# A graph network on one core: the edge weights' part on VectorE from a broadcast load, and a bias row on TensorE instead of a second node table

## The chip, the core and the metric

The kernel runs on one core of one Trainium2 chip. The core has five engines that run side by side: PE (TensorE, matrix products), DVE (VectorE), ACT (ScalarE), POOL (GpSimd, which here only issues indirect DMA transfers, "gathers") and SP (SyncE, which issues the plain DMA transfers). They wait for one another by semaphores. The metric is the device time of one execution in microseconds (us); lower is better.

## The reference, cut to what matters

There are 50,000 nodes with 128 features, 25,000 edges sorted by their target, and four layers one behind the other. The change touches the first layer and the second convolution of the second layer.

```python
# first layer: ew is one number per edge
ef  = concat([x[src], x[dst], ew[:, None]])           # 128 + 128 + 1
msg = leaky_relu(ef @ W_edge + b_edge)                # slope 0.01
red = segment_sum(msg, dst)
x1  = layernorm(x + leaky_relu(concat([x, red]) @ W_node + b_node))
# second layer: two convolutions with attention, then again a residual and a layernorm
h1  = relu(conv(x1, q0, k0, v0, s0))
x2  = layernorm(x1 + conv(h1, q1, k1, v1, s1))        # conv ends with "+ h @ s_w + s_b"
```

## The kernel before

Edges and nodes are padded to 49 tiles; a tile is 512 edges and, beside them, two blocks of 512 nodes. Features lie on the 128 partitions once a block has been transposed by PE. The program is a row of stages with a barrier between them: `setup`, `layer0`, `conv` 0, `conv` 1, `layer2`, `layer3`. Each stage is a loop over 49 steps plus a few to drain, written out in full; the order of the instructions on each engine is the order in which the step function writes them, and every dependence is a semaphore wait written by hand.

**`setup`** loads the weights, computes the row numbers by which later stages gather, and prepares constants. Its DVE part ends in a chain in which each instruction waits for the one before (`link`). Line 318 centres the bias row of the second convolution (`s_b1c`, broadcast over the 128 partitions).

**`layer0`**, step `t`, with tile `now` = t and older tiles behind it:
- PE (line 602 on) transposes the node rows `xn`, then forms `psZ`, the messages before the activation, from three products: `w_src` (L614), `w_dst` (L615), and `w_edge_row` times `erow` (L616). The last one adds the edge weights' part: `erow` is a tile of zeros with the 512 edge weights in its first row, and `w_edge_row` has the weight row in its first row. Then come the transposes of the next tile's gathered rows `xd` and `xs`, the node products L624, `centred` products `psE` of `tT` (L589), `centred` of `psZ` for an older tile, and the edge products L640 and L642.
- ACT copies, squares and scales; `y01` (L696, shown as `y`) follows L642, and `z01` (L676, shown as `z` in the rows) is 0.01 times `psZ` plus a bias.
- DVE: `lr` (L712, the leaky ReLU of the products), `tT` (L717 and L721, plus the input), `msg` (L727, the leaky ReLU of `psZ`), the running sum `red` (L732), the sum of squares `var` (L441), `rstd` times a mask (L744), the output `xo` (L749), and `xb` (L756). `xb` is `xo` of the two node blocks plus `s_b1c`.
- SP loads `xn` and `erow` of coming tiles, stores `xo` to the table `x1` and `xb` to a second node table, `x1b`.
- POOL issues per step four gathers of `xs` for the tile three ahead and some 3.2 of `xd` (196 in all, 48 of them issued already in `setup`); each is one quarter of a tile.

**`conv`, layer 1** (the second convolution): `own_rows` (L940) forms `psE[k]` = h1 times `s1c` for the two node blocks, and DVE's `add_x1` (L1165) adds the residual, which SP loads from `x1b` (with the bias in it) for nodes. PE's order in a step is: transposes of `xs` and `xd`, query product, transposes of the nodes, key product (L1003), values `psV` (L953), `own_rows` for both blocks, `alike` `psA` (L958, needs DVE's `kq`), and `edge_products` (L947, L948).

Of the kernel before, what the change touches and what calls it, by code (L numbers as in the profile page):

```python
# [129 lines left out]
def setup(nc, io, h):  # L130

    with ExitStack() as ctx:
# [10 lines left out]
        dst1 = sb("dst1", [P, COLS])  # L143
        src1, src1_rows = sb("src1", [P, COLS]), sb("src1_rows", [HALF, 2 * P])
# [60 lines left out]
        def _(act):  # L205
# [10 lines left out]
            load(h.w_edge_row[0:1, :], io["w_edge_row"])  # L216
# [6 lines left out]
        def _(dve):  # L223
# [283 lines left out]
def layer0(nc, io, h):  # L507


    with ExitStack() as ctx:  # L510
# [8 lines left out]
        erow = sb("erow", [P, 2, TILE])  # L519
# [4 lines left out]
        xo, xb = sb("xo", [P, 2, 3, TILE]), sb("xb", [P, 2, 2, TILE])  # L524
        psT, psZ, psY, psE = ps("psT", 2), ps("psZ", 1), ps("psY", 3), ps("psE", 2)
        node_landed, erow_landed, node_stored, edge_stored, xb_stored = [
            [sem(f"{n}{s}") for s in range(2)] for n in (
                "node_landed", "erow_landed", "node_stored", "edge_stored", "xb_stored")]
        (e_turned, n_turned, e_kept, n_kept, erow_zero, z_ready, z01_ready, msg_ready, red_ready, yn_ready, ye_ready,
         y01_ready, lr_ready, te_ready, tn_ready, ee_ready, en_ready, ce_ready, cn_ready, sq_ready, var_ready,  # L530
         lnv_ready, rstd_ready, out_ready, xb_ready, masked, last_landed) = map(sem, (
             "e_turned", "n_turned", "e_kept", "n_kept", "erow_zero", "z_ready", "z01_ready", "msg_ready", "red_ready",
             "yn_ready", "ye_ready", "y01_ready", "lr_ready", "te_ready", "tn_ready", "ee_ready", "en_ready",
             "ce_ready", "cn_ready", "sq_ready", "var_ready", "lnv_ready", "rstd_ready", "out_ready", "xb_ready", "masked",
# [20 lines left out]
        def _(sp):  # L555
            sp.wait_ge(erow_zero, 1)
# [20 lines left out]
            for s in range(2):  # L577
                sp.wait_ge(xb_stored[s], 16 * tiles_in_slot(s))

        @block.tensor  # L580
        def _(pe):
# [18 lines left out]
            def step(t):  # L600
                soon, now, last, old = t.tile(-1), t.tile(0), t.tile(1), t.tile(2)
                if now:
# [30 lines left out]
                if old:  # L633
                    pe.wait_ge(te_ready, old.n + 1)
                    wait(pe, msg_ready, old.n + 3 if now else STEPS)
                    centred(psZ[:, 0, :], tT[:, 2, :]).then_inc(ee_ready, 1)
# [11 lines left out]
        def _(act):  # L648
# [7 lines left out]
            def step(t):  # L656
# [16 lines left out]
                if now:  # L673
                    act.wait_ge(z_ready, now.n + 1)
                    wait(act, msg_ready, now.n)
                    nc.scalar.activation(z01[:, :], psZ[:, 0, :], ACT.Identity, bias=h.x01b_edge[:, :],  # L676
# [25 lines left out]
        def _(dve):  # L702
            nc.vector.memset(erow[:, :, :], 0.0).then_inc(erow_zero, 1)

            def step(t):
                now, last, old = t.tile(0), t.tile(1), t.tile(2)
                (g, a, b), (g2, a2, b2), (g3, a3, b3) = t.group(1), t.group(2), t.group(3)
                if g:
# [5 lines left out]
                    dve.wait_ge(lr_ready, g.n + 1)  # L714
                if last:
# [7 lines left out]
                if now:  # L723
# [3 lines left out]
                    nc.vector.scalar_tensor_tensor(out=msg[:, :], in0=psZ[:, 0, :], scalar=h.col("b_edge"),  # L727
# [1404 lines left out]
```

## Time and profile before

| | us |
|---|---|
| median of three timed runs | 3164.38 (3162.36 to 3165.82) |
| the profiled execution | 3169.91 |
| its span, first to last instruction | 3168.1 |
| `layer0` in it, from the first PE instruction at 135.97 to the barrier before `conv` 0 at 679.2 | 543 |
| period of one step in `layer0` and in `conv` 1 | 10.44 and 11.34 |

| engine | busy us | share of the span |
|---|---|---|
| PE | 2503.6 | 79% |
| DVE | 2587.8 | 82% |
| ACT | 2089.9 | 66% |
| POOL | 1869.3 | 59% |

No engine bounds the whole program. Each stage has its own limit, so the stage's timeline is what is to be read: instructions in order of time, with how long the engine stood idle before one and who released it. An instruction's recorded time includes its way through the pipeline, so the next one on the engine can start some 0.1 us before the last one's recorded end.

### The profile page before, as it was taken

How to read it: one execution, taken by the hardware profiler on the slowest of the kernel's cores; microseconds unless marked ns; L12 is line 12 of the kernel's file. 1: busy time of each engine (PE TensorE's matmuls, PEld its weight loads, DVE VectorE, ACT ScalarE, POOL GpSimd, SP SyncE). 2: the span in 40 equal slices, each digit the busy share in tenths (PEclk: the TensorE clock that was granted, in tenths of full speed). 3: DMA queues.
4: the chain of work that ended last, by engine and by line, in shares of the span. 5: the costliest groups of instructions: out<-in, count | busy, mean ns of one | idle time of the engine just before them, and what ended most of it. 6: DMA issues, size and time to landing. Idle time of an engine off the chain costs nothing. (4 is left out here: it accounts for less than half of the span.)

```text
span 3168.1 us, 46332 instructions
## 1 busy us (share of the span) xinstructions
PE 2503.6 (79%) x14131; PEld 1745.7 (55%) x14131; DVE 2587.8 (82%) x3230; ACT 2089.9 (66%) x3726; POOL 1869.3 (59%) x1771
## 2 busy tenths in 40 slices
PE   7899999959999968888888699999999753345500
PEld 3466666637677756666665466777777542234400
DVE  6689999969999959999999457898888747999900
ACT  0176767746666648888888589999999744545500
POOL 4477777723344427777775556555555007777776
PEclk9999999979999989999999899999999855666855
DMA  7456767657677756777776448888988538984211
GB/s 210 114 176 222 222 217 229 214 167 219 207 215 220 216 161 209 231 233 233 232 232 206 118 138 212 217 210 206 236 213 213 153 101 275 277 275 136 81 40 39
DMA packets 495087, 611.79 MB, mean 193 GB/s; under 512 B 66865, under 2 KB 284651, under 8 KB 494716
## 3 DMA queue, kind: packets, MB, share of 16 engines
q1 hardware_dynamic: 433030, 495.63, 52.0%
q0 software_dynamic: 56480, 111.88, 13.6%
q8 instruction: 118, 1.93, 0.3%
q10 hardware_dynamic: 5334, 1.32, 0.2%
q14 instruction: 125, 1.02, 0.1%
HBM read 391.94 MB, written 220.55 MB: 193 GB/s over the span
## 5 line engine op out<-in xcount | busy, mean ns | idle before, releaser
L1848 POOL DMA_INDIRECT f_rows<-table_x,src_row x196 | 228.9, 1168 | 225.2 <-POOLq L1249 165.8
L1328 POOL DMA_INDIRECT g_xd_xs<-table_x,dst_row x196 | 199.0, 1015 | 263.9 <-PE g_psT L1396 170.1
L781 POOL DMA_INDIRECT c_xs<-table_x,src_row x196 | 187.3, 956 | 261.9 <-PE c_psT L923 209.4
L771 POOL DMA_INDIRECT c_xs<-table_h,src_row x196 | 221.3, 1129 | 121.4 <-issue 78.9
L503 POOL DMA_INDIRECT xs<-in_x,src_i x196 | 227.1, 1159 | 86.6 <-issue 55.5
L488 POOL DMA_INDIRECT xd<-in_x,dst_i x196 | 216.9, 1106 | 94.8 <-issue 47.6
L1328 POOL DMA_INDIRECT g_xd_xs<-table_x,src_row x196 | 205.0, 1046 | 59.7 <-issue 59.7
L1855 POOL DMA_INDIRECT out<-f_rows,end_i x196 | 197.1, 1006 | 62.4 <-issue 62.1
L1900 PE MATMUL f_psT<-w_ident,f_rows 128*128 128x128 f32 x196 | 48.5, 393 | 219.9 <-DVE f_rows L1993 219.9
L771 POOL DMA_INDIRECT c_xd<-table_h,dst_row x196 | 185.1, 944 | 59.7 <-issue 59.7
L1401 PEld LDWEIGHTS g_psP<-w_center,g_turns 128*128 128x128 f32 x1568 | 183.8, 191 | 49.6 <-ACT g_turns L1537 28.3
L1401 PE MATMUL g_psP<-w_center,g_turns 128*128 128x128 f32 x1568 | 197.2, 279 | 7.5 <-ACT g_turns L1566 4.7
L1032 ACT ACTIVATE c_xo<-c_pre,c_rstd 128x128 f32<-128x128 f32 x588 | 182.0, 388 | 1.6
L1900 PEld LDWEIGHTS f_psT<-w_ident,f_rows 128*128 128x128 f32 x196 | 30.9, 195 | 232.1 <-DVE f_rows L1993 232.1
L1401 PE MATMUL g_psU<-w_center,g_turns 128*128 128x128 f32 x784 | 124.7, 310 | 38.6 <-ACT g_turns L1542 25.7
L1924 ACT ACTIVATE f_sqe<-f_rows 128x512 f32<-128x512 f32 x49 | 30.9, 630 | 166.5 <-DVE f_vare L1970 146.2
L1401 PEld LDWEIGHTS g_psU<-w_center,g_turns 128*128 128x128 f32 x784 | 111.8, 220 | 46.0 <-ACT g_turns L1542 31.8
L953 PE MATMUL c_psV<-c_xsT,w_v 128*128 128x512 f32 x196 | 105.3, 619 | 35.5 <-DVE c_pv L1207 35.5
L1729 DVE TENSOR_TENSOR g_pre<-g_psP,g_xn 128x1024 f32<-128x1024 f32 x49 | 59.9, 1223 | 87.4 <-ACT g_n L1523 52.6
L1179 DVE TENSOR_TENSOR_SCAN c_m<-far,c_m,c_psA 128x512 f32<-128x512 bf16 x98 | 124.6, 1271 | 1.6 <-PE c_psA L958 1.6
L1213 DVE TENSOR_TENSOR_SCAN c_den<-c_c,c_den,c_p 128x512 f32<-128x512 f32 x96 | 122.2, 1273 | 0.0
L1219 DVE TENSOR_TENSOR_SCAN c_num<-c_c,c_num,c_pv 128x512 f32<-128x512 f32 x96 | 120.6, 1256 | 0.0
(338 smaller groups left out, 8457.2 us busy)
## 6 DMA issues: line engine op xcount, KB each, us to landing
g_share<-shares SPq DMA_DIRECT2D x196, 192.0 KB
xn<-in_x SPq DMA_DIRECT2D x49, 512.0 KB
table_x<-xo SPq DMA_DIRECT2D x49, 512.0 KB, 2.9
table_x1b<-xb SPq DMA_DIRECT2D x49, 512.0 KB, 4.9
c_xn<-table_x SPq DMA_DIRECT2D x49, 512.0 KB
table_h<-c_xo SPq DMA_DIRECT2D x49, 512.0 KB
c_xn<-table_h SPq DMA_DIRECT2D x49, 512.0 KB
c_x1r<-table_x1b SPq DMA_DIRECT2D x49, 512.0 KB
```

Source lines behind the costliest of these rows:

```text
L488: pool.indirect_dma_start(out=quarters(h.xd0[:, s, :])[j], out_offset=None, in_=io["x0"], in_offset=edge_index(h.dst_i, n, j)).then_inc(h. ...
L503: pool.indirect_dma_start(out=quarters(h.xs0[:, s, :])[j], out_offset=None, in_=io["x0"], in_offset=edge_index(h.src_i, n, j)).then_inc(h. ...
L771: pool.indirect_dma_start(out=quarters(rows[:, s, :])[j], out_offset=None, in_=table, in_offset=edge_index(columns, now.n, j)).then_inc(la ...
L781: pool.indirect_dma_start(out=quarters(xs[:, s, :])[j], out_offset=None, in_=table, in_offset=edge_index(h.src_row, now.n, j)).then_inc(sr ...
L1032: ins = nc.scalar.activation(quarters(xo[:, g.slot, j // 4, :])[j % 4], quarters(pre[:, g.slot, j // 4, :])[j % 4], ACT.Copy, scale=rstd[: ...
L1179: nc.vector.tensor_tensor_scan(m[:, s, 1:TILE + 1], h.far[:, here], psA[:, :], m[:, s, 0:1], ALU.add, ALU.max).then_inc(m_ready, 1)
L1213: nc.vector.tensor_tensor_scan(den[:, s, :], c[:, :], p[:, :], 0.0 if first else den[:, 1 - s, TILE - 1:TILE], ALU.mult, ALU.add).then_inc ...
L1219: nc.vector.tensor_tensor_scan(num[:, s, :], c[:, :], pv[:, :], 0.0 if first else num[:, 1 - s, TILE - 1:TILE], ALU.mult, ALU.add).then_in ...
L1328: pool.indirect_dma_start(out=quarters(xd_xs[:, s, k, :])[j], out_offset=None, in_=table, in_offset=edge_index(columns, now.n, j)).then_in ...
L1401: ins = nc.tensor.matmul(o, x, h.w["center"][:, :], start=True, stop=True)
L1848: pool.indirect_dma_start(out=quarters(rows[:, n, :])[j], out_offset=None, in_=table, in_offset=edge_index(h.src_row, n, j)).then_inc(src_ ...
L1855: pool.indirect_dma_start(out=io["out"], out_offset=edge_index(h.end_i, n, j), in_=quarters(rows[:, n, :])[j], in_offset=None, bounds_chec ...
```

## The change

In `layer0` the third product L616 goes, and with it `erow`, the zeroed tiles and the wait for their zeroing. SP instead loads the 512 edge weights broadcast to all 128 partitions (`ew`, 256 KB in SBUF), and a new DVE instruction makes `z` = `ew` times the weight column plus `psZ`. It stands behind `lr` and before `tT`. ACT's `z01` and DVE's `msg` now read `z` in SBUF instead of `psZ` in PSUM. The instruction `xb`, its store and the table `x1b` go.

In `conv` 1 the residual is loaded from `x1`. The bias comes from a PE product in front of each block's `own_rows` products: a 3 x 128 tile of ones times `bias3`, a 3 x 512 tile in bf16 that holds the centred bias row in three bf16 parts that add up to it (each repeated four times). Nine new linked DVE instructions in `setup` split the row into these parts.

```diff
@@ setup, vector
-            nc.vector.memset(h.w_edge_row[:, :], 0.0)
+            nc.vector.memset(h.ones3[:, :], 1.0)
+            bias_left, parts_sum = h.s_b1c, ew1[:, 0:P]
+            for k in range(3):
+                link(nc.vector.tensor_copy(bias_part[:, :], bias_left[:, :]))
+                if k < 2:
+                    link(nc.vector.tensor_tensor(h.s_b1c[:, :], h.s_b1c[:, :], bias_part[:, :], ALU.subtract))
+                place_in = h.w["ident"][:, k:k + 1]
+                if k == 0:
+                    link(nc.vector.tensor_scalar(parts_sum, bias_part[:, :], place_in, None, ALU.mult))
+                else:
+                    link(nc.vector.scalar_tensor_tensor(out=parts_sum, in0=bias_part[:, :], scalar=place_in,
+                                                        in1=parts_sum, op0=ALU.mult, op1=ALU.add))
+            link(nc.vector.tensor_copy(by_row(h.bias3[:, :]), parts_sum[0:3, :].rearrange(
+                "p (o f) -> p o f", o=1).to_broadcast([3, 4, P])))
@@ layer0, sync
-            sp.wait_ge(erow_zero, 1)
             sp.dma_start(h.last_flat, h.dst_row[P - 1:P, :]).then_inc(last_landed, 16)
...
-                    wait(sp, z_ready, now.n - 1)
-                    sp.dma_start(erow[0:1, s, :], io["ew"][:, bass.ds(now.n * TILE, TILE)]).then_inc(erow_landed[s], 16)
+                    wait(sp, z_added, now.n - 1)
+                    sp.dma_start(ew[:, s, :], io["ew"][:, bass.ds(now.n * TILE, TILE)].to_broadcast([P, TILE])
+                                 ).then_inc(ew_landed[s], 16)
                 store_group(sp, g, a, b, t, x1, xo, out_ready, node_stored, edge_stored)
-                if g and a == 0:
-                    sp.wait_ge(xb_ready, g.n + 1)
-                    sp.dma_start(node_rows(io["x1b"], g.n), xb[:, g.slot, :, :]).then_inc(xb_stored[g.slot], 16)
@@ layer0, tensor
-                    nc.tensor.matmul(psZ[:, 0, :], h.w["w_dst"][:, :], edgeT[:, e, 0, :], start=False, stop=False)
-                    nc.tensor.matmul(psZ[:, 0, :], h.w_edge_row[:, :], erow[:, now.slot, :],
+                    nc.tensor.matmul(psZ[:, 0, :], h.w["w_dst"][:, :], edgeT[:, e, 0, :],
                                      start=False, stop=True).then_inc(z_ready, 1)
@@ layer0, scalar
-                    nc.scalar.activation(z01[:, :], psZ[:, 0, :], ACT.Identity, bias=h.x01b_edge[:, :],
+                    nc.scalar.activation(z01[:, :], z[:, :], ACT.Identity, bias=h.x01b_edge[:, :],
@@ layer0, vector
-            nc.vector.memset(erow[:, :, :], 0.0).then_inc(erow_zero, 1)
...
+                if now:
+                    dve.wait_ge(z_ready, now.n + 1)
+                    dve.wait_ge(ew_landed[now.slot], 16 * (now.half + 1))
+                    wait(dve, z01_ready, now.n)
+                    nc.vector.scalar_tensor_tensor(out=z[:, :], in0=ew[:, now.slot, :], scalar=h.w_edge_col[:, :],
+                                                   in1=psZ[:, 0, :], op0=ALU.mult, op1=ALU.add).then_inc(z_added, 1)
...
-                    nc.vector.scalar_tensor_tensor(out=msg[:, :], in0=psZ[:, 0, :], scalar=h.col("b_edge"),
+                    nc.vector.scalar_tensor_tensor(out=msg[:, :], in0=z[:, :], scalar=h.col("b_edge"),
...
-                        nc.vector.tensor_tensor(wide(xb[:, g3.slot, :, :]), wide(xo[:, g3.slot, 0:2, :]),
@@ conv, sync and tensor
-                        sp.dma_start(x1r[:, u0.slot, 0:2, :], node_rows(io["x1b"], now.n)).then_inc(x1n_landed[now.slot], 16)
+                        sp.dma_start(x1r[:, u0.slot, 0:2, :], node_rows(io["x1"], now.n)).then_inc(x1n_landed[now.slot], 16)
...
-                    ins = nc.tensor.matmul(o, x, w_own[:, :], start=True, stop=True)
+                if layer:
+                    nc.tensor.matmul(psE[k][:, :], h.ones3[:, :], h.bias3[:, :], start=True, stop=False)
+                for j, (o, x) in enumerate(zip(quarters(psE[k]), quarters(xnT[:, now.slot, k, :]))):
+                    ins = nc.tensor.matmul(o, x, w_own[:, :], start=not layer, stop=not layer or j == 3)
```

How the order changes is shown at three places. On DVE, in one step of `layer0`, this stands before (out, then what is read, then the shape; `y` is `y01` or `z01`, see above):

```order
L712 SCALAR_TENSOR_TENSOR lr<-psY,cols,y 128x1536
L717 TENSOR_TENSOR tT<-lr,nodeT 128x1024
L721 TENSOR_TENSOR tT<-lr,edgeT 128x512
L727 SCALAR_TENSOR_TENSOR msg<-psZ,cols,z 128x512
L732 SCALAR_TENSOR_TENSOR red<-cont,red,msg 128x512
L441 TENSOR_REDUCE var<-sq 128x12
L744 TENSOR_TENSOR rstd<-rstd,ends 128x4
L749 TENSOR_TENSOR xo<-cen,rstd 128x1536
L756 TENSOR_TENSOR xb<-xo,s_b1c 128x1024
```

and this stands in the changed kernel (its line numbers are shifted):

```order
L717 SCALAR_TENSOR_TENSOR lr<-psY,cols,y 128x1536
L724 SCALAR_TENSOR_TENSOR z<-ew,w_edge_col,psZ 128x512
L728 TENSOR_TENSOR tT<-lr,nodeT 128x1024
L732 TENSOR_TENSOR tT<-lr,edgeT 128x512
L738 SCALAR_TENSOR_TENSOR msg<-z,cols 128x512
L743 SCALAR_TENSOR_TENSOR red<-cont,red,msg 128x512
L455 TENSOR_REDUCE var<-sq 128x12
L755 TENSOR_TENSOR rstd<-rstd,ends 128x4
L760 TENSOR_TENSOR xo<-cen,rstd 128x1536
```

`xb` has gone from the end of the step and `z` has come in between `lr` and `tT`. On PE, in the same step, before and then now:

```order
L584 MATMUL psT<-w_ident,xn 128x128 x8
L614 MATMUL psZ<-edgeT,w_w_src 128x512
L615 MATMUL psZ<-edgeT,w_w_dst 128x512
L616 MATMUL psZ<-erow,w_edge_row 128x512
L584 MATMUL psT<-w_ident,xd 128x128 x4
```

```order
L593 MATMUL psT<-w_ident,xn 128x128 x8
L622 MATMUL psZ<-edgeT,w_w_src 128x512
L623 MATMUL psZ<-edgeT,w_w_dst 128x512
L593 MATMUL psT<-w_ident,xd 128x128 x4
L593 MATMUL psT<-w_ident,xs 128x128 x4
```

One 512-column product less; the rest is as it was. On PE in `conv` 1, between the values and the edge products, before and then now:

```order
L953 MATMUL c_psV<-c_xsT,w_v 128x512
L940 MATMUL c_psE<-s1c,c_xnT 128x128 x8
L958 MATMUL c_psA<-c_kq,w_heads 128x512
L947 MATMUL c_psE<-w_center,c_agg 128x128
L948 MATMUL c_psE<-s1c,c_xdT 128x128
```

```order
L959 MATMUL c_psV<-c_xsT,w_v 128x512
L944 MATMUL c_psE<-bias,ones 128x512
L946 MATMUL c_psE<-s1c,c_xnT 128x128 x4
L944 MATMUL c_psE<-bias,ones 128x512
L946 MATMUL c_psE<-s1c,c_xnT 128x128 x4
L964 MATMUL c_psA<-c_kq,w_heads 128x512
L953 MATMUL c_psE<-w_center,c_agg 128x128
```

Two bias products have come in ahead of `alike`.

## Rows read from the trace of the kernel before

**Rows 1.** busy us by engine in a stretch (x instructions), clock, DMA share

```profile
300.00:400.00 100.00, 100.00 (x523) 67.39 (x522) 98.54 (x88) 69.79 (x88) 79.31 (x68) 1.00 0.70 222
```

**Rows 2.** timeline, one step of `layer0`, PE: start us, us, line, names

```profile
406.53 1.95 PE L589 MATMUL psE<-w_center,tT 128*128 128x128 f32 x16
...
410.06 1.02 PE L642 MATMUL psY<-red,w_w_red 128*128 128x512 f32 x2
...
410.92 1.04 PE L584 MATMUL psT<-w_ident,xn 128*128 128x128 f32 x8
```

**Rows 3.** timeline, the same step: DVE, and ACT's `y01`

```profile
402.31 1.82 DVE L712 SCALAR_TENSOR_TENSOR lr<-psY,cols,y 128x1536 f32<-128x1536 f32 x1
...
404.16 1.23 DVE L717 TENSOR_TENSOR tT<-lr,nodeT 128x1024 f32<-128x1024 f32 x1
...
405.30 0.69 DVE L721 TENSOR_TENSOR tT<-lr,edgeT 128x512 f32<-128x512 f32 x1
...
405.90 0.75 DVE L727 SCALAR_TENSOR_TENSOR msg<-psZ,cols,z 128x512 f32<-128x512 f32 x1
...
406.69 1.28 DVE L732 TENSOR_TENSOR_SCAN red<-cont,red,msg 128x512 f32<-128x512 uint8 x1
...
411.17 1.55 ACT L696 ACTIVATE y<-psY,x01b_node 128x1536 f32<-128x1536 f32 x1 [1.09 <-issue]
...
411.51 1.22 DVE L756 TENSOR_TENSOR xb<-xo,s_b1c 128x1024 f32<-128x1024 f32 x1
...
412.75 1.82 DVE L712 SCALAR_TENSOR_TENSOR lr<-psY,cols,y 128x1536 f32<-128x1536 f32 x1
```

**Rows 4.** timeline, DVE, two later steps of `layer0`

```profile
486.10 1.82 DVE L712 SCALAR_TENSOR_TENSOR lr<-psY,cols,y 128x1536 f32<-128x1536 f32 x1 [0.28 <-ACT y L696]
...
496.44 1.81 DVE L712 SCALAR_TENSOR_TENSOR lr<-psY,cols,y 128x1536 f32<-128x1536 f32 x1
```

**Rows 5.** timeline, POOL, the same step as rows 2

```profile
404.67 1.54 POOL L503 DMA_INDIRECT xs<-in_x,src_i  x1 [0.30 <-issue]
...
406.51 0.94 POOL L503 DMA_INDIRECT xs<-in_x,src_i  x1 [0.30 <-issue]
...
410.27 2.02 POOL L488 DMA_INDIRECT xd<-in_x,dst_i  x1 [0.30 <-DMA xd<-in_x,dst_i]
```

**Rows 6.** timeline, end of `layer0`, POOL's last gather, then PE's last tile

```profile
625.75 0.94 POOL L488 DMA_INDIRECT xd<-in_x,dst_i  x1 [0.30 <-issue]
...
633.61 0.60 PE L584 MATMUL psT<-w_ident,xd 128*128 128x128 f32 x4
```

**Rows 7.** timeline, start of `layer0`: DVE's zeroing, SP's first transfer, PE's first product

```profile
136.06 0.91 DVE L703 MEMSET erow<- 128x1024 f32 x1 [1.85 <-PEq L132]
...
137.00 0.25 SPq L557 DMA_DIRECT2D last_flat<-dst_row  x1
...
144.22 1.92 PE L614 MATMUL psZ<-edgeT,w_w_src 128*128 128x512 f32 x2
```

**Rows 8.** page, DMA issues: KB each, us from issue to landing

```profile
table_x<-xo SPq DMA_DIRECT2D x49, 512.0 KB, 2.9
...
table_x1b<-xb SPq DMA_DIRECT2D x49, 512.0 KB, 4.9
```

**Rows 9.** timeline, DVE in the chain of `setup`

```profile
127.92 0.29 DVE L318 TENSOR_SCALAR s_b1c<-s_b1c,i_rowm 128x128 f32<-128x128 f32 x1
```

**Rows 10.** timeline, one step of `conv` 1, PE and DVE's `kq`

```profile
1507.57 1.95 PE L940 MATMUL c_psE<-s1c,c_xnT 128*128 128x128 f32 x16
...
1508.84 0.72 DVE L1154 SCALAR_TENSOR_TENSOR c_kq<-c_psQ,cols,c_q 128x512 f32<-128x512 f32 x1
...
1509.62 1.12 PE L958 MATMUL c_psA<-c_kq,w_heads 128*128 128x512 f32 x2
...
1510.58 0.38 PE L947 MATMUL c_psE<-w_center,c_agg 128*128 128x128 f32 x2
```

**Rows 11.** groups of PE: bf16 products of 512 columns in `setup`

```profile
L378 PE MATMUL i_psb<-i_at_or_past,i_blocks 98*128 98x512 bf16 x196 | 91.4, 623 | 7.9 <-DVE i_at_or_past L276 7.9
```

More of the change, by code:

```diff
@@ L215, in _ @@
             act.wait_ge(rows_zero, 1)
-            load(h.w_edge_row[0:1, :], io["w_edge_row"])
+            load(h.w_edge_col[:, :], io["w_edge_row"].rearrange("o p -> p o"))
             load(h.w_e_row[0:1, :], io["w_e_row"])
@@ L518, in layer0 @@
         xn, nodeT = sb("xn", [P, 2, 2, TILE]), sb("nodeT", [P, 2, 2, TILE])
-        erow = sb("erow", [P, 2, TILE])
+        ew, z = sb("ew", [P, 2, TILE]), sb("z", [P, TILE])
         z01, msg, red = sb("z01", [P, TILE]), sb("msg", [P, TILE]), sb("red", [P, 2, TILE])
@@ L610, in step @@
                     ins.then_inc(n_turned, 1)
-                    pe.wait_ge(erow_landed[now.slot], 16 * (now.half + 1))
                     wait(pe, ce_ready, now.n - 2)
-                    wait(pe, msg_ready, now.n)
+                    wait(pe, z_added, now.n)
                     nc.tensor.matmul(psZ[:, 0, :], h.w["w_src"][:, :], edgeT[:, e, 1, :], start=True, stop=False)
-                    nc.tensor.matmul(psZ[:, 0, :], h.w["w_dst"][:, :], edgeT[:, e, 0, :], start=False, stop=False)
-                    nc.tensor.matmul(psZ[:, 0, :], h.w_edge_row[:, :], erow[:, now.slot, :],
+                    nc.tensor.matmul(psZ[:, 0, :], h.w["w_dst"][:, :], edgeT[:, e, 0, :],
                                      start=False, stop=True).then_inc(z_ready, 1)
@@ L634, in step @@
                     pe.wait_ge(te_ready, old.n + 1)
-                    wait(pe, msg_ready, old.n + 3 if now else STEPS)
+                    wait(pe, z_added, old.n + 3 if now else STEPS)
                     centred(psZ[:, 0, :], tT[:, 2, :]).then_inc(ee_ready, 1)
@@ L751, in step @@
                                             scale, ALU.mult).then_inc(out_ready, 1)
-                    if a3 == 0:
-                        dve.wait_ge(out_ready, g3.n + 1)
-                        wait(dve, xb_stored[g3.slot], 16 * g3.half)
-                        wide = lambda x: by_row(x.rearrange("p b n -> p (b n)"))
-                        nc.vector.tensor_tensor(wide(xb[:, g3.slot, :, :]), wide(xo[:, g3.slot, 0:2, :]),
-                                                h.s_b1c[:, :].rearrange("p (o f) -> p o f", o=1).to_broadcast([P, 8, P]),
-                                                ALU.add).then_inc(xb_ready, 1)
             run_steps(4, step)
@@ L938, in own_rows @@
                 wait(pe, pren_ready if layer else out_ready, 2 * now.n - 1 + k)
-                for o, x in zip(quarters(psE[k]), quarters(xnT[:, now.slot, k, :])):
-                    ins = nc.tensor.matmul(o, x, w_own[:, :], start=True, stop=True)
+                if layer:
+                    nc.tensor.matmul(psE[k][:, :], h.ones3[:, :], h.bias3[:, :], start=True, stop=False)
+                for j, (o, x) in enumerate(zip(quarters(psE[k]), quarters(xnT[:, now.slot, k, :]))):
+                    ins = nc.tensor.matmul(o, x, w_own[:, :], start=not layer, stop=not layer or j == 3)
                 ins.then_inc(en_ready, 1)
@@ L2026, in build @@
         h.s_b0, h.s_b1c, h.s0_lifted = square("s_b0"), square("s_b1c"), square("s0_lifted")
-        h.w_edge_row, h.w_e_row = square("w_edge_row"), square("w_e_row")
+        h.w_edge_col, h.w_e_row = column("w_edge_col"), square("w_e_row")
         h.b_vs = sb("b_vs", [P, 2])
+        h.ones3, h.bias3 = sb("ones3", [3, P], BF16), sb("bias3", [3, TILE], BF16)
         h.x01b_node, h.x01b_edge = column("x01b_node"), column("x01b_edge")
@@ L2035, in build @@
         h.ends, h.last_row = sb("ends", [P, COLS]), sb("last_row", [STEPS, 4], I32)
-        io["x1b"] = nc.dram_tensor("table_x1b", (NODE_ROWS, P), F32, kind="Internal").ap()
         h.src1_flat = nc.dram_tensor("src1_flat", (1, EDGE_ROWS), F32, kind="Internal").ap()
```

19 lines of the change are left out of this document (9 added, 10 removed).

## The prediction, made before the changed kernel ran

> **What bounds the kernel now.** I read the busy time per stage first, then the timelines of one step in the two stages that the change touches. In `layer0` PE is busy 100.00 of 100 us and DVE 98.54, at the full granted clock [rows 1]. The timeline says which of them leads. PE goes without a gap: L642 starts at 410.06 and the next step's transposes at 410.92, so a 512-column f32 product occupies 0.86 (its record of 1.02 has a tail of 0.16) [rows 2]. DVE looks full too, `lr` to `lr` is 412.75 - 402.31 = 10.44, but when it is late it can make a step in 496.44 - 486.10 = 10.34 [rows 3, 4]. So PE sets 10.44 and DVE has 0.10 to spare. POOL is never idle for more than 0.30, but that is no bound as long as PE doesn't wait for a gather: PE turns the last tile at 633.61, 7.9 us after POOL's last gather begins at 625.75 [rows 6]. In `conv` 1 the step is 11.34 and a chain across the engines bounds it; its last part is `kq` on DVE, `psA`, then the edge products on PE [rows 10].
>
> **PE's product in `layer0` goes.** It has L642's shape: 0.86 off PE's step, which would leave 10.44 - 0.86 = 9.58. PE was the bound, so this is on the path, and the question is what is late next.
>
> **DVE in `layer0`.** `xb` goes: 1.22, of which the next instruction could overlap 0.09 (`tT` of 1.23 is followed after 1.14), so 1.13, and 0.12 more because `xb` stands 0.03 behind the recorded end of `xo` that it reads, instead of 0.09 ahead of it [rows 3]. `z` comes: the same shape and kind as `msg`, 0.75, so 0.66 after overlap. DVE alone would need 10.34 - 1.25 + 0.66 = 9.75.
>
> **The order of `z` is what decides.** It stands behind `lr` and in front of `tT`, and PE's `psE` needs `tT`. This closes a chain around three engines. From L642 to `y01`: 411.17 - 410.06 = 1.11. `y01` to `lr`: 412.75 - 411.17 = 1.58. `lr` to the next DVE instruction: 404.16 - 402.31 = 1.85. `z`: 0.66. `tT`: 1.23, and 0.16 until PE's products stream (`kq` is over at 1509.56 and `psA`, which takes 0.86 and is followed at 1510.58, effectively began at 1509.72). `psE` to L642: 410.06 - 406.53 = 3.53 [rows 2, 3, 10]. The sum is 1.11 + 1.58 + 1.85 + 0.66 + 1.39 + 3.53 = 10.12. Without `z` it is 9.46, which the 10.44 of before hides. PE would come to `psE` 0.5 us before `tT` is there. Two of the links may be some 0.05 shorter when the engine really waits; I take **10.10 per step** (10.00 to 10.15), a gain of 0.34. Some 46.5 steps run at this period: 15.8 us (13.5 to 20.5).
>
> **Start and end of `layer0`.** SP's first transfer stands at 137.00, right behind the zeroing of `erow` that ends at 136.97 (136.06 + 0.91) [rows 7]; without it SP begins with the others, 1.1 earlier, and the first `xn` lands so much earlier. The first two steps are filling, and PE's missing products (at the start one takes 1.92 instead of 1.02 [rows 2, 7]) come out whole or nearly so, where later steps give 0.34: some 1.4 more. Together 2.5. In the drain four `xb` of 1.22 stand in DVE's queue, three of them in front of something the end waits for, one partly beside a wait: 2.7 (1.5 to 3.7). The last store is now one to `x1`, 2.9 us to landing where `x1b` took 4.9 [rows 8]: between 0 and 2, I take 1.0, as the two transfers share the queue.
>
> **Transfers.** Per step 512 KB of `x1b` go and 256 KB of `ew` come. SP issues `ew` for the tile after the one in work, about a step ahead, so I cost it at nothing; were it later than 8 us, `z` and everything behind it on DVE would wait. Nothing is queued behind SP's wait for `z` but stores that come later anyway.
>
> **POOL.** Its period is locked to DVE's: seven gathers a step, of which two are stretched. The one that starts at 404.67 lasts 1.54 and ends 0.82 after the first `tT`, the one at 410.27 lasts 2.02 and ends 0.78 after `xo` (which is over as `xb` starts), while one under `lr` or `var` takes 0.94 or so [rows 3, 5]. A gather that starts while DVE reads two SBUF operands waits for that instruction. With a shorter step I count again seven per step: after `xo`, three (the third caught by `tT` for 0.2), then the first behind `tT`, then two, then the one caught by `xo`. So POOL speeds up with the rest, but its lead at the start doesn't grow; the 7.9 us at the end shrink to some 4, of which a landing takes 2 to 4. I put 0.5 (0 to 1.5) for a wait of PE there.
>
> **Setup.** Nine linked DVE instructions are added in a chain that ends in the barrier, with nothing beside it to hide them. Eight are like L318, 0.29 and 0.03 for the link [rows 9]; the ninth has 512 columns on three partitions, up to 0.69 as the `tT` of 512 columns [rows 3]. Copies to bf16 may be cheaper. 8 x 0.32 + 0.5 = **3.1** (2.4 to 3.4), a loss.
>
> **`conv` 1.** Two bf16 products of 512 columns per step stand before `psA`. Their price at full clock is in no row. In `setup` one took 0.62 on record, 0.46 without the tail [rows 11], at a time when PE ran at half its later rate: at the start of `layer0` an f32 product took 1.92, later 1.02 [rows 2, 7]. Halved it is 0.23, the two 0.45; unhalved, 0.92. Not all of that is on the path: `own_rows` starts at 1507.57 and takes 1.78 (its record of 1.95 less the tail), so PE is free at 1509.35 while `psA` begins at 1509.72 because it waits for `kq` [rows 10]. 0.37 is covered. At 0.45 a step grows by 0.08, with a little for the change of type 0.09: 48 steps and the fill make **4.4** (3 to 7).
>
> The TensorE page of the Trainium skill ("TensorE: Matmul & The Clock Gate", Part 1) gives N / 2.4 GHz + 2.5 ns per warm product, 215.7 ns at N = 512; by it the two cost 0.43 and the term would be 3.4, not 4.4. No row of this trace has a bf16 product of this width at the full clock.
>
> **The sum** against the profiled run of 3169.91: -15.8 - 2.5 - 2.7 - 1.0 + 0.5 + 3.1 + 4.4 = -14.0. That run is one execution, 5.5 us above the median of the timed runs; the difference is carried to the median: 3164.4 - 14.0 = **3150.4**. About 0.2% (6.3 us) is what a measurement of this kernel can tell from no change.
>
> **Rivals.**
> (A) The bias products cost 0.46 each, as recorded in `setup`. Then a step of `conv` 1 grows by 0.92 - 0.37 = 0.55, 26.6 us instead of 4.4, and the kernel takes 3172.6, slower by 8. It decides from 0.37 for the pair upward; break-even is at 0.66. For it: it is the only bf16 row. Against it: the halved rate of that time.
> (B) The step of `layer0` stays at 10.44, because some link that I don't see takes up what PE gives back (the gathers, the broadcast load): -14.0 + 15.8 = +1.8, 3166. For it: POOL has no idle time at all. Against: its stretches are waits for DVE that move with DVE.
> (C) `z` turns out not to be in the way and only DVE's own work counts, 9.75: another 0.35 x 46.5 = 16.3, 3134. Against: the order of the instructions is fixed.
> (D) POOL falls to six gathers a step. `msg` now reads two SBUF operands and directly precedes the scan `red`, which also does. Before, a gather started at 406.51, 0.18 before the scan at 406.69, and went through in 0.94 [rows 3, 5]. If it is held under `msg` and then loses to the scan, it waits 1.3 more, and one gather fewer fits. `layer0` issues 332 gathers (392 less 60 in `setup`), some 296 of them in the locked part: at 10.10 / 6 = 1.68 each instead of 10.10 / 7 = 1.44, 71 us more, less some 5 of slack: 3216. It decides when that gather starts later than the scan, 0.18 us. Against: at the two boundaries seen, `tT` to `tT` and `xo` to `xb`, the waiting gather went first.
>
> The page "SBUF — State Buffer" of the Trainium skill, section "Who interferes with whom", says that an instruction with two SBUF inputs blocks a GpSimd instruction that reads SBUF, and infers that the issue of a transfer isn't stalled by such a tensor_tensor. By that inference D could not happen; the stretched gathers speak against the inference.
>
> **Chances.** The forecast 0.70, with 3141 to 3158 as its own range; A 0.07, B 0.08, C 0.07, D 0.04, and 0.04 for what I have not thought of. The range from 3139 to 3166 holds the forecast and B and leaves out A, C and D. Faster: the forecast and C, 0.77; same: B and the edges, 0.13; slower: A, D and a part of the unknown, 0.10.
>
> **What would show it.** In `layer0`: `lr` to `lr` 10.1; DVE `z` of 0.75 right behind `lr`; PE idle about 0.5 per step, most of it before `psE`, released by `tT`; POOL still seven gathers per step. In `setup`: nine new rows, 3 us. In `conv` 1: L944 at about 0.23, `psA` no longer waiting for `kq`, a step of 11.42. It is wrong if PE's wait in `layer0` is for something else than DVE's `lr` or `tT`, or if `conv` 1 grows by more than 7 us.

## The result and the profile after

The changed kernel takes 3181.3 us (3178.4 to 3184.9), the kernel before 3165.8 (3162.4 to 3167.7) beside it: ratio 1.005, interval 1.0035 to 1.0064. It is **slower by 15.5 us**, where 14 us faster was forecast. Both halves show in the trace, one as forecast, one not.

The first table sets the stages of the two profiled runs (spans 3168.1 and 3179.8) against each other. A boundary is the first instruction of a stage on ACT, right behind the barrier.

| stretch | forecast | in the traces |
|---|---|---|
| up to the start of `conv` 0 (`setup` and `layer0`) | -18.4 | -16.6 |
| `conv` 0 | 0 | -6.2 |
| `conv` 1 | +4.4 | +32.7 |
| the rest | 0 | +1.8 |

The first of these boundaries, before and after:

```profile
679.23 1.28 ACT L1015 ACT_TABLE_LOAD   x1 [8.98 <-PEq L2041]
```

```profile
662.61 1.28 ACT L1021 ACT_TABLE_LOAD   x1 [7.56 <-PEq L2047]
```

**`layer0`.** The window 300 to 400 of after, busy us by engine (compare [rows 1]):

```profile
300.00:400.00 100.00, 99.05 (x511) 63.60 (x511) 96.03 (x90) 73.53 (x88) 78.96 (x70) 1.00 0.64 200
```

One step of `layer0` in after: start us, length us, engine, line, names, and in brackets the wait ahead of it and its releaser (compare [rows 2, 3]):

```profile
404.56 1.82 DVE L717 SCALAR_TENSOR_TENSOR lr<-psY,cols,y 128x1536 f32<-128x1536 f32 x1 [0.29 <-ACT y L703]
...
406.42 0.75 DVE L724 SCALAR_TENSOR_TENSOR z<-ew,w_edge_col,psZ 128x512 f32<-128x512 f32 x1
...
407.08 1.22 DVE L728 TENSOR_TENSOR tT<-lr,nodeT 128x1024 f32<-128x1024 f32 x1
...
408.35 1.86 PEld L598 LDWEIGHTS psE<-w_center,tT 128*128 128x128 f32 x16 [0.70 <-DVE tT L728]
...
409.60 1.28 DVE L743 TENSOR_TENSOR_SCAN red<-cont,red,msg 128x512 f32<-128x512 uint8 x1
...
411.14 1.02 PE L647 MATMUL psY<-edgeT,w_w_node 128*128 128x512 f32 x2
...
414.69 1.82 DVE L717 SCALAR_TENSOR_TENSOR lr<-psY,cols,y 128x1536 f32<-128x1536 f32 x1 [0.29 <-ACT y L703]
```

`lr` to `lr` is 414.69 - 404.56 = 10.13, on the average 10.12. `z` (L724) stands between `lr` and the first `tT`, PE's weight load for `psE` waits 0.70 for that `tT`, and from there it goes over L647 and `y01` (L703) back to `lr`, which waits 0.29 for it. This is the chain of the forecast, link by link.

**`setup`.** The last instruction of DVE's chain before, then the same in after, and SP's first transfer of `layer0` (compare [rows 7]):

```profile
133.84 0.36 DVE L349 CAST dst_row<-i_psr 128x196 int32<-128x196 f32 x1 [1.11 <-PE i_psr L420]
```

```profile
136.69 0.36 DVE L363 CAST dst_row<-i_psr 128x196 int32<-128x196 f32 x1 [1.11 <-PE i_psr L434]
```

```profile
138.23 0.25 SPq L570 DMA_DIRECT2D last_flat<-dst_row  x1
```

With the nine new instructions the chain's last one starts 2.85 later. SP begins 138.23 - 137.00 = 1.2 later than before: it no longer waits for the zeroing of `erow`, which gives back 1.6.

**`conv` 0** isn't touched, yet it is 6.2 shorter. From the first to the last `kq` of `conv` 0 the kernel before took 453.5, after 446.3, and the kernels below, whose `conv` 0 does the same, 443.8 to 451.9. Behind the first one, the steps of before there vary from 8.96 to 13.1. The kernel before has only this one profile, and it is of a long execution (3169.9 against a median of 3165.8). So the difference is probably not the change, though a single profile can't show that. Without it the balance is -16.6 + 32.7 + 1.8 = +17.9, against 15.5 between the medians, for which the interval leaves room from 11 to 20.

**`conv` 1.** One step of after (compare [rows 10]):

```profile
1502.78 1.13 PE L959 MATMUL c_psV<-c_xsT,w_v 128*128 128x512 f32 x2 [0.74 <-DVE c_pv L1213]
...
1503.84 0.38 PE L944 MATMUL c_psE<-bias,ones 3*128 3x512 bf16 x1
...
1504.15 1.16 PE L946 MATMUL c_psE<-s1c,c_xnT 128*128 128x128 f32 x8
...
1505.01 0.73 DVE L1160 SCALAR_TENSOR_TENSOR c_kq<-c_psQ,cols,c_q 128x512 f32<-128x512 f32 x1
...
1505.24 0.39 PE L944 MATMUL c_psE<-bias,ones 3*128 3x512 bf16 x1
...
1505.56 1.16 PE L946 MATMUL c_psE<-s1c,c_xnT 128*128 128x128 f32 x8
...
1506.55 1.02 PE L964 MATMUL c_psA<-c_kq,w_heads 128*128 128x512 f32 x2
...
1509.40 0.69 DVE L1171 TENSOR_TENSOR c_pre<-c_psE,c_x1r 128x512 f32<-128x512 f32 x1 [0.50 <-PE c_psE L954]
...
1518.56 1.02 PE L964 MATMUL c_psA<-c_kq,w_heads 128*128 128x512 f32 x2
```

`psA` to `psA` is 12.01, before 11.34. Between `psV` and `psA` there are now two bias products (L944), each recorded with 0.38 or 0.39, and `psA` doesn't wait for `kq` any more (`kq` is over at 1505.74). DVE's third `c_pre` (L1171), which never waited, waits 0.5 us in each step for PE's edge products.

### The profile page after: what moved, and what is told of

Read it like the earlier page. It is cut to its first block and busy times, and to the rows that moved or that the text cites. A ratio compares the mean times of both kernels' runs of the same rounds, so it can differ in the third digit from the quotient of the medians.

```text
span 3179.8 us, 46291 instructions
## 1 busy us (share of the span) xinstructions
PE 2521.2 (79%) x14131; PEld 1726.6 (54%) x14131; DVE 2568.1 (81%) x3238; ACT 2097.0 (66%) x3726; POOL 1869.3 (59%) x1771
## 5 line engine op out<-in xcount | busy, mean ns | idle before, releaser
L502 POOL DMA_INDIRECT xd<-in_x,dst_i x196 | 210.4, 1074 | 94.8 <-issue 47.2
L1171 DVE TENSOR_TENSOR c_pre<-c_psE,c_x1r 128x512 f32<-128x512 f32 x147 | 96.9, 686 | 30.6 <-PE c_psE L954 28.1
```

The source lines that it names most:

```text
L502: pool.indirect_dma_start(out=quarters(h.xd0[:, s, :])[j], out_offset=None, in_=io["x0"], in_offset=edge_index(h.dst_i, n, j)).then_inc(h. ...
```

## The experiments

The first theory after the result was that the two bias products alone lengthen `conv` 1. Four kernels take them out, halve them, put them together and make them narrow. Of the last three there is one execution each (3157.8, 3164.3 and 3172.9 us), too few to compare times that differ by some us elsewhere in the program; the step of `conv` 1 repeats to about 0.01, so it is the steps that are compared. In the fences of this part the columns are those above, PE only, one step of `conv` 1.

**Without the bias products**

```diff
-                if layer:
-                    nc.tensor.matmul(psE[k][:, :], h.ones3[:, :], h.bias3[:, :], start=True, stop=False)
-                for j, (o, x) in enumerate(zip(quarters(psE[k]), quarters(xnT[:, now.slot, k, :]))):
-                    ins = nc.tensor.matmul(o, x, w_own[:, :], start=not layer, stop=not layer or j == 3)
+                for o, x in zip(quarters(psE[k]), quarters(xnT[:, now.slot, k, :])):
+                    ins = nc.tensor.matmul(o, x, w_own[:, :], start=True, stop=True)
```

> The changed kernel with both bias products of conv 1 left out (the bias isn't added at all; psE is written by the f32 products alone, as before). Theory P (the two bias products stand on the path and cost 0.97 us in PE's order, of which 0.30 was covered by the wait for kq): the step of conv 1 falls from 12.01 back to 11.34, and the kernel from 3181.3 to about 3149. Rival L (it is the residual rows, read from x1 instead of x1b, or another access of conv 1 that grew): the step stays at 12.0 and the kernel at 3181.

```profile
1504.62 1.12 PE L957 MATMUL c_psV<-c_xsT,w_v 128*128 128x512 f32 x2 [0.74 <-DVE c_pv L1211]
1505.59 1.95 PE L944 MATMUL c_psE<-s1c,c_xnT 128*128 128x128 f32 x16
1507.63 1.12 PE L962 MATMUL c_psA<-c_kq,w_heads 128*128 128x512 f32 x2
...
1518.99 1.12 PE L962 MATMUL c_psA<-c_kq,w_heads 128*128 128x512 f32 x2
```

The kernel leaves out the bias. 3146.9 us, ratio 0.9936 (0.9919 to 0.9953); the step is 11.36 here, 11.34 on the average. The whole loss of `conv` 1 hangs on the two products. From `psV` to the first product of `own_rows` it is 0.97 without a bias.

**One of the two**

```diff
-                if layer:
+                biased = layer and k == 0
+                if biased:
...
-                    ins = nc.tensor.matmul(o, x, w_own[:, :], start=not layer, stop=not layer or j == 3)
+                    ins = nc.tensor.matmul(o, x, w_own[:, :], start=not biased, stop=not biased or j == 3)
```

> The changed kernel with the bias product of psE[0] only (the second node half gets no bias). Theory P: one product is 0.49 in PE's order, 0.30 of it covered by the wait for kq: step of conv 1 11.34 + 0.19 = 11.53. Rival N (no cover, the step grows with each product from the first on): half of 0.67, 11.68.

```profile
1501.49 1.12 PE L960 MATMUL c_psV<-c_xsT,w_v 128*128 128x512 f32 x2 [0.74 <-DVE c_pv L1214]
1502.55 0.39 PE L945 MATMUL c_psE<-bias,ones 3*128 3x512 bf16 x1
1502.87 2.05 PE L947 MATMUL c_psE<-s1c,c_xnT 128*128 128x128 f32 x16
1504.76 1.02 PE L965 MATMUL c_psA<-c_kq,w_heads 128*128 128x512 f32 x2
...
1516.26 1.02 PE L965 MATMUL c_psA<-c_kq,w_heads 128*128 128x512 f32 x2
```

The step is 11.50. Here `psA` doesn't wait, so the 16 products of `own_rows` and the change to `psA` take 1504.76 - 1502.87 = 1.89. Without a bias, then, `psV` to `psA` would be 0.96 + 1.89 = 2.85. Before, it is 0.96 and the 1509.72 - 1507.57 = 2.15 of the forecast [rows 10], together 3.11, because `psA` waits for `kq`: **0.26 is covered**. The one bias product makes it 3.27, so it costs 0.42 (0.41 on the average), and the step grows by 3.27 - 3.11 = 0.16.

**Both side by side**

```diff
                     values(now)
+                    bias_rows(now, 0)
+                    bias_rows(now, 1)
                     own_rows(now, 0)
```

`bias_rows` is the product of L944 with its wait for `psE[k]`, taken out of `own_rows`.

> The changed kernel with the two bias products of conv 1 side by side, behind psV and ahead of both blocks of f32 products. Theory S (a bf16 product streams in about 0.22, and 0.25 to 0.3 is the break between f32 and bf16, paid once for each run of bf16 products): one pair of breaks goes, step 12.01 - 0.25 = 11.76. Rival W (each product costs 0.49 by its own width, wherever it stands): 12.01.

```profile
1505.13 1.12 PE L961 MATMUL c_psV<-c_xsT,w_v 128*128 128x512 f32 x2 [0.74 <-DVE c_pv L1217]
1506.19 0.60 PE L941 MATMUL c_psE<-bias,ones 3*128 3x512 bf16 x2
1506.72 2.05 PE L948 MATMUL c_psE<-s1c,c_xnT 128*128 128x128 f32 x16
1508.61 1.02 PE L966 MATMUL c_psA<-c_kq,w_heads 128*128 128x512 f32 x2
...
1520.33 1.02 PE L966 MATMUL c_psA<-c_kq,w_heads 128*128 128x512 f32 x2
```

The step is 11.72. From L941 to L948 it is 0.53 for two products, where one took 0.32.

**Narrow**

```diff
-                    nc.tensor.matmul(psE[k][:, :], h.ones3[:, :], h.bias3[:, :], start=True, stop=False)
+                    nc.tensor.matmul(psE[k][:, 0:P], h.ones3[:, :], h.bias3[:, 0:P], start=True, stop=False)
...
-                    ins = nc.tensor.matmul(o, x, w_own[:, :], start=not layer, stop=not layer or j == 3)
+                    ins = nc.tensor.matmul(o, x, w_own[:, :], start=not layer or j > 0, stop=True)
```

Three quarters of the columns get no bias here, and their f32 products don't add to anything.

> The changed kernel with bias products of 128 columns instead of 512 (three quarters of the rows' nodes get no bias). Theory S (0.22 of stream and 0.27 of breaks for each product): three quarters of the stream go, 2 x 0.16 = 0.32 less, step 11.69. Rival W (0.49 is all stream): 2 x 0.37 less than 0.97 leaves 0.23, which the wait for kq covers, step 11.34.

```profile
1501.16 0.22 PE L944 MATMUL c_psE<-bias,ones 3*128 3x128 bf16 x1
1501.32 1.16 PE L946 MATMUL c_psE<-s1c,c_xnT 128*128 128x128 f32 x8
...
1503.56 1.02 PE L964 MATMUL c_psA<-c_kq,w_heads 128*128 128x512 f32 x2
...
1515.25 1.02 PE L964 MATMUL c_psA<-c_kq,w_heads 128*128 128x512 f32 x2
```

The step is 11.69: 2 x 384 columns less save 12.01 - 11.69 = 0.32. That is 0.42 ns per column, so a product of 512 columns streams in 0.21. The blocks of `own_rows` take as long as in after, though now one product in four adds to the bias where all four did: adding isn't what costs. The page "TensorE: Matmul & The Clock Gate" of the Trainium skill (Part 1) has 215.7 ns for it. The trace agrees, with 0.21 us, and the price that was too small in the forecast wasn't this one.

**What a bf16 product between f32 products costs** comes out of these four:

- `psV` to the next product is 0.96 if that is f32, 1.06 if it is the bias: 0.10 ahead.
- A bias product to the next f32 product is 0.31 or 0.32, of which 0.21 are stream: 0.10 behind.
- Two blocks of eight take 1.09 - 0.10 and 0.99, together 1.98, one block of sixteen 1.89: 0.09 because the second bias product cuts the block in two.

So the pair costs 2 x (0.10 + 0.21 + 0.10) + 0.09 = 0.91, and after's own rows say 3.77 - 2.85 = **0.92**. Side by side it is 0.63 (3.48 - 2.85), which is about 2 x 0.21 and one pair of breaks. Less the cover of 0.26 this makes 0.66 and 0.37 per step; measured were 0.67 and 0.38. What the 0.10 consist of isn't shown: the change of type and the change from 128 contraction rows to 3 always come together here.

**In PE's waits.** PE waits 0.74 for `xdT` ahead of `psQ` and 0.74 for `pv` ahead of `psV`, before and after. By then `psE[0]` and `psE[1]` have been free for some 2 us.

```diff
                     turn(1, now, xd[:, s, :], dst_landed[s], 64 * (now.half + 1))
+                    bias_rows(now, 0)
...
+                    bias_rows(now, 1)
                     values(now)
```

> The changed kernel with the same two bias products of conv 1 moved into waits of PE: that of psE[0] behind the transposes of xd, where PE waits 0.74 us or more for xdT, that of psE[1] behind the k product, where PE waits 0.74 for pv. Nothing is left out. Theory S (a product is 0.22 of stream and 0.27 of breaks, 0.49 in all, and a wait of 0.74 covers it): step of conv 1 11.34, kernel as without the bias, 3147 to 3149. Rival B (the breaks are paid behind the wait, as the next f32 product starts late after a bf16 product that is long over): 11.34 + 2 x 0.1 to 0.27, up to 11.9, kernel 3150 to 3174.

```profile
1499.99 0.38 PE L941 MATMUL c_psE<-bias,ones 3*128 3x512 bf16 x1
1500.80 1.12 PE L1008 MATMUL c_psQ<-c_xdT,w_q 128*128 128x512 f32 x2 [0.42 <-ACT c_xdT L1099]
...
1503.80 0.38 PE L941 MATMUL c_psE<-bias,ones 3*128 3x512 bf16 x1
1504.61 1.12 PE L961 MATMUL c_psV<-c_xsT,w_v 128*128 128x512 f32 x2 [0.42 <-DVE c_pv L1217]
```

3146.5 us, ratio 0.9945 (0.9931 to 0.9959), step 11.34: as fast as without the bias. Both products run at the start of a wait, and 0.42 of each wait is left; nothing of the breaks falls behind it. This version is faster than both kernels. A second time, beside the kernels that follow:

> The kernel with the bias products of conv 1 in PE's two waits, once more, beside the next one and against the kernel before: 3146 to 3147, ratio 0.9945, step of layer0 10.12, of conv 1 11.34.

3148.7 us, ratio 0.9948 (0.9934 to 0.9962).

**Both in one wait**, that for `pv`:

> Both bias products of conv 1 in one wait, that of 0.74 for pv, side by side. Theory S (two products of 0.22 and one pair of breaks of about 0.27, in all 0.70): the wait just covers them, step 11.34 to 11.40. If the breaks fall behind the wait instead: 11.34 + 0.27 = 11.6.

```profile
1507.14 0.60 PE L941 MATMUL c_psE<-bias,ones 3*128 3x512 bf16 x2
1507.95 1.13 PE L961 MATMUL c_psV<-c_xsT,w_v 128*128 128x512 f32 x2 [0.21 <-DVE c_pv L1217]
```

The step is 11.35, and 0.21 of the wait is left: the pair took 0.53 of it.

**The other half alone.** `layer0` has PE's product again and no `z`; `x1b` and its additions are gone, `conv` 1 is as changed:

```diff
+                    nc.tensor.matmul(psZ[:, 0, :], h.w_edge_row[:, :], erow[:, now.slot, :],
...
-                    nc.vector.scalar_tensor_tensor(out=z[:, :], in0=ew[:, now.slot, :], scalar=h.w_edge_col[:, :],
-                                                   in1=psZ[:, 0, :], op0=ALU.mult, op1=ALU.add).then_inc(z_added, 1)
```

> The second half of the change alone: layer0 has PE's product with the edge weights' row again and no z on DVE, but the table x1b and the xb additions are gone, and conv 1 adds the bias as changed. Theory PE (before, PE was the bound of layer0, and xb's 1.22 us on DVE lay beside it): step of layer0 10.44 as before. Rival D (DVE was the bound, or its xb held up the chain): near 10.34 - 1.25 = 9.1 for DVE, so the step falls to PE's floor, seen as a value below 10.4.

3195.6 us in one execution, step of `layer0` 10.44, of `conv` 1 12.01. Taking DVE's `xb` away brings nothing in the step: PE, with its product, was the bound. The kernel is 14.3 us above after.

**`z` behind the first `tT`.** The chain of `layer0` holds `z`; without it 9.46 was the sum. The two statements of DVE change places:

```diff
-                if now:
-                    dve.wait_ge(z_ready, now.n + 1)
...
                 if last:
                     wait(dve, en_ready, last.n)
                     nc.vector.tensor_tensor(tT[:, 0:2, :], lr[:, 0:2, :], nodeT[:, last.slot, :, :],
                                             ALU.add).then_inc(tn_ready, 1)
+                if now:
+                    dve.wait_ge(z_ready, now.n + 1)
...
```

> The changed kernel with z of layer 0 issued behind the first tT instead of ahead of it; conv 1 as changed. Theory Z (the 10.12 is the chain y01, lr, z, tT, psE, psY, and z is the link in it that need not be there; then DVE's own work of 9.75 or PE's 9.58 bounds): step of layer0 9.75 to 9.85, kernel 3181.3 - 46.5 x 0.32 = 3166. Rival P (POOL with its seven gathers a step is full, 7 x 0.30 idle and the stretched ones, and nothing shortens): 10.12 and 3181; or PE waits for gathers and the end comes later, 3186.

```profile
302.06 1.29 DVE L743 TENSOR_TENSOR_SCAN red<-cont,red,msg 128x512 f32<-128x512 uint8 x1
...
302.21 1.89 POOL L517 DMA_INDIRECT xs<-in_x,src_i  x1 [0.30 <-issue]
...
305.10 1.76 DVE L760 TENSOR_TENSOR xo<-cen,rstd 128x1536 f32<-128x1536 f32 x1
...
305.65 2.02 POOL L502 DMA_INDIRECT xd<-in_x,dst_i  x1 [0.30 <-issue]
...
309.22 1.43 POOL L517 DMA_INDIRECT xs<-in_x,src_i  x1 [0.30 <-issue]
```

3229.9 us, ratio 1.0207 (1.0191 to 1.0223), slower than anything else here. The step is 10.01 as a rule, because `msg` now waits 0.19 for `z01` and DVE is otherwise full, but about every fourth or fifth takes 13 to 17, and the last scan of `layer0` comes 48.7 us later than in after (681.16 instead of 632.47). The rows (POOL's gathers, DVE's scan `red` L743 and `xo` L760) say why. `red` starts at 302.06, the gather 0.15 later, and it is held until the scan is over: 1.89. In after the gather starts at 409.43 and the scan at 409.60 (its row is in the step of after, above), so the gather is 0.17 ahead, and it takes 0.96:

```profile
409.43 0.96 POOL L517 DMA_INDIRECT xs<-in_x,src_i  x1 [0.31 <-issue]
```

The one at 305.65 is caught by `xo`, that at 309.22 by `tT`, and six gathers fit into a step instead of seven. PE's line in the list of waits, 200 to 600 us (total, times, longest):

```profile
PE psT L593 <- DMA xs<-in_x,src_i: 31.6, 11, 3.8
```

**Both moves at once**, the bias products in PE's waits and `z` behind `tT`:

> Both moves at once: the bias products of conv 1 in PE's waits and z behind the first tT. The candidate for a version faster than both kernels. By theories S and Z: 3148 - 15 = 3133. If Z fails 3148, if S fails 3150 to 3166.

3203.8 us, ratio 1.0116 (1.0100 to 1.0131), with the same long steps. The loss and the gain add up to within 9 us: 3181.3 + 48.6 - 34.8 = 3195.1.

**The scan taken out.** To see whether the gather is held by the scan and not late by itself:

```diff
-                    nc.vector.tensor_tensor_scan(red[:, s, :], h.cont[:, bass.ds(now.n * TILE, TILE)], msg[:, :],
-                                                 first, ALU.mult, ALU.add).then_inc(red_ready, 1)
+                    nc.vector.tensor_reduce(red[:, s, 0:4], by_row(msg[:, :]), AX_X, ALU.add)
+                    nc.vector.tensor_reduce(red[:, s, 4:8], by_row(msg[:, :]), AX_X, ALU.add).then_inc(red_ready, 1)
```

> z behind the first tT as in the slow run, and the scan red (two SBUF operands, 1.28 us) replaced by two reductions of msg with one operand each (about 0.58 each); so the running sum isn't computed and red holds no sums. Theory G (in the slow run a gather that started 0.15 behind the scan was held 1.89 us, POOL came to six gathers a step, and PE waited 5 to 6 us for a gather every fourth or fifth step): without the scan a gather in that place takes 0.95, seven fit, and the steps of 15 to 17 us are gone: layer0 at 9.8 to 10.1 per step throughout, kernel 3165 to 3178. Rival M (the gathers are late for another reason: landing, queue, or the shorter step itself): steps of 15 us stay, kernel above 3210.

```profile
306.10 0.69 DVE L747 TENSOR_REDUCE red<-msg 128x4 f32<-128x512 f32 x1
...
306.25 0.95 POOL L502 DMA_INDIRECT xd<-in_x,dst_i  x1 [0.30 <-issue]
```

The kernel leaves out the running sum. 3178.1 us in one execution. The gather starts 0.15 behind DVE's instruction as before, but that one reads a single operand, and it takes 0.95. Seven fit, `z` to `z` is 10.02 to 10.04 from the fifth step to the last but for one of 10.25, and the long steps are gone. That it is the operands and not the scan as such is seen in after: there 41 gathers start 0.21 to 0.24 behind `z` (0.75 long), which reads one operand from SBUF (`ew`) and one from PSUM (`psZ`), and none is held:

```profile
406.65 0.94 POOL L502 DMA_INDIRECT xd<-in_x,dst_i  x1 [0.31 <-issue]
```

**The bias split moved.** The nine linked DVE instructions go from `setup` to the start of `conv` 0, ahead of DVE's wait for the first transposed rows, with `pv` for the sum:

```diff
             if spread:
+                bias_left, parts_sum = h.s_b1c, pv[:, 0:P]
+                for k in range(3):
+                    link(nc.vector.tensor_copy(bias_part[:, :], bias_left[:, :]))
...
                 dve.wait_ge(last_turned, 1)
```

> The same kernel with the nine linked DVE instructions that split the bias moved out of setup to the start of conv 0, where DVE waits about 6 us for the first gathers. Theory H (in setup they stand in a chain with nothing beside it, 2.85 us; in conv 0 the wait hides them): 2.9 us less, 3143.6. Rival K (setup's end is set by something else too, or DVE's wait at the start of conv 0 is on the path): no change, 3146.5.

3144.2 us, ratio 0.9932 (0.9918 to 0.9946), 4.5 less than the version without the move on the same chip, where 2.9 was expected; the two intervals overlap.

**The last gather.** In five of the ten profiled runs with `z` ahead of `tT` and 60 gathers in `setup`, the last step of `layer0` took 15.2 to 15.6 instead of 10.1. POOL's last gather and PE's transposes of it, in after and then in the kernel with the narrow products:

```profile
614.58 0.95 POOL L502 DMA_INDIRECT xd<-in_x,dst_i  x1 [0.30 <-DMA xd<-in_x,dst_i]
```

```profile
615.87 2.02 POOL L502 DMA_INDIRECT xd<-in_x,dst_i  x1 [0.30 <-DMA xd<-in_x,dst_i]
...
622.28 1.11 PE L593 MATMUL psT<-w_ident,xd 128*128 128x128 f32 x4 [3.99 <-DMA xd<-in_x,dst_i]
```

In the runs without the long step the last gather starts 2.3 behind the third last scan and is through in 0.95. In the five others it starts 3.6 behind it, one slot of 1.25 later, and there `xo` catches it for 2.02. The time needed for it to land is then not there, and PE waits 4 us. POOL issues seven gathers in a step and needs 7.2 (392 less the 60 of `setup`, over 46 steps), so its lead melts to nothing just at the end. One more kernel has four more gathers in `setup`, beside the same without them:

```diff
-ROW_SLOTS, EARLY_TILES = 3, 12
+ROW_SLOTS, EARLY_TILES = 3, 13
```

> The kernel with the bias products in PE's waits and the bias split at the start of conv 0, and in addition 64 gathers instead of 60 issued during setup (13 tiles of xd ahead instead of 12). Theory Q (POOL issues seven gathers a step but needs 7.2, so its lead melts until the last tile; where it had issued 18 or 19 gathers instead of 20 by the first scan red, the last gather is caught by xo for 2.02 us, lands late and the last step takes 15.2 instead of 10.1): with four more ahead the last step is 10.12 in the profile and the kernel at the lower end of the one without, 3140 to 3144. Rival T (the extra gathers lengthen setup, or the last step's wait has another cause): 3144 to 3149, last step 15 or setup 2 to 5 us longer.

> The kernel of the run before this one without the four extra gathers, for comparison on the same chip: 3144, ratio 0.993. By theory Q its last step of layer0 is 15 us if 18 or 19 gathers were issued by the first scan, 10.1 if 20.

```profile
605.46 0.94 POOL L488 DMA_INDIRECT xd<-in_x,dst_i  x1 [0.30 <-issue]
```

3142.4 us, ratio 0.9916 (0.9901 to 0.9931), against 3145.4 and 0.9927 (0.9911 to 0.9942). The last gather now starts 2.9 ahead of the third last scan (608.41), no step is long. The profiled run without it had a short last step too, its gather in the early slot. The slot is settled at the start. Counted from the kernel's first gather, 68 have begun ahead of the first scan in the five runs with the long step and 69 in the five without, and the one gather less is still missing at the end. The counts of 18 to 20 in the text on record don't tell the runs apart; this one does. So the cause of the long step is shown by its rows, but what the four gathers bring to the median, some 3 us, isn't told apart from nothing by these intervals.

## Why the prediction was wrong, point by point

- **`layer0`, the chain with `z`: right.** 10.12 was the sum, 10.12 is measured; 10.10 was taken. Putting PE's product back gives 10.44. The links are as forecast: `tT` releases `psE`, PE's wait is 0.70 in the load queue, DVE is busy 96.03 of 100.
- **Start, end and `setup`: right within 2 us.** Everything ahead of `conv` 0 was put at -18.4 and is -16.6. From the first scan to the last (149.93 to 646.80 before, 151.01 to 632.47 after) it is -15.4, where -15.8 for the steps and -1.4 for the filling were forecast; 10.12 instead of 10.10 makes 0.9 of that. From the last scan to the barrier it is -2.3, where -3.2 was. The nine rows cost 2.85 (forecast 3.1), SP's earlier start gives 1.6 (forecast 1.1). That a gather may come late at the end was put at 0.5 (0 to 1.5); it is 0 in half of the runs and some 5 in the others.
- **The term of `conv` 1: the step that failed.** The forecast was 4.4 us, measured 32.7. Three sizes stand in it. The stream of a product, 0.23 at full rate, was right (0.21). "With a little for the change of type", 0.01 per step, is wrong: the pair has four breaks of 0.10 and one of 0.09, 0.49 in all. And the cover wasn't 0.37 but 0.26: the 1.78 for `own_rows` was the record less its tail, but where `psA` doesn't wait it comes 1.89 behind the start of the block. So a step grows by 0.92 - 0.26 = 0.66 instead of 0.45 - 0.37 = 0.08; 48 of them are 31.7, and the fill makes the rest of 32.7. The break-even on record, 0.66 for the pair, is also wrong: it was taken from the whole -14.0, in which the 4.4 of `conv` 1 is already counted. From the -18.4 of the other terms it is 18.4 / 48 + 0.37 = 0.75.
- **Rival A** had the right price for the pair, 0.92, by luck: its reason (a product at half rate) is wrong, and so is its cover. It gave 26.6 us and 3172.6. Its only price, the 0.46 of `setup` [rows 11], is of bf16 products among other bf16 products, at half of PE's later rate. The chance of 0.07 rested on halving it, and the halving is right for the stream and says nothing of the breaks. With D's 0.04 it makes 0.11, so the 0.10 for slower was a little under the forecast's own parts.
- **Rival D** didn't come for the change, but its mechanism and its deciding point are real. It decided by "when that gather starts later than the scan, 0.18 us": in after the gather is 0.17 ahead and goes through, with `z` moved it is 0.15 behind and POOL falls to six gathers a step, 48.7 us in `layer0`. Its other premise, that `msg` with two SBUF operands would hold the gather, didn't come: the gather starts only when 0.15 of `msg` is left and takes 0.96. The page "SBUF — State Buffer" of the Trainium skill, section "Who interferes with whom", infers that a tensor_tensor doesn't hold up the issue of a transfer. The gathers of 2.02 under the TENSOR_TENSOR `xo` speak against it, and those of 1.89 under the scan, against 0.95 with one-operand reductions in its place, say the same of a scan.
- **Rival C** (9.75 if `z` isn't in the way) is 10.01 where `z` is out of the chain: DVE waits 0.19 for `z01`, and DVE's own work is 9.82 there. POOL wouldn't have allowed much less anyway: in the kernel without the scan its seven gathers a step, two of them stretched (1.72 and 1.44), fill 10.0 with their gaps of 0.30.

## What to carry to other kernels

A small product of another type between f32 products costs its breaks first and its columns second: here 0.41 us for 0.21 of stream, more if it cuts a block. Before it is put on the path, look for a wait of its engine: the same two products are free a few lines earlier in the program. And before the order on VectorE is improved, look at which of its instructions the gathers meet: one of them 0.15 us on the wrong side of a scan cost more than the whole change could bring.

## What the hardware showed that was not expected

- A bf16 product of 512 columns and 3 contraction rows between f32 products: 0.10 us ahead, 0.21 stream, 0.10 behind; in a run of two the breaks are paid once.
- A gather issued 0.15 us behind the start of a VectorE instruction with two SBUF operands is held to its end (0.95 becomes 1.89 under a scan of 1.28), one issued 0.17 ahead isn't (0.96), nor one issued 0.2 behind the start of an instruction whose second operand is in PSUM (0.94).
- The untouched `conv` 0 differs by up to 10 us between the profiled runs (443.8 to 453.5 from its first to its last `kq`), two thirds of what this change was to bring.
